# Two-layer graph network on one core: layer 2's load of the kept rows moved from SyncE's list to GpSimd's

## What is computed

```
h   = relu(layernorm(x))
w   = two-layer network on the edge features      # 192 weights per edge
msg = products of w, h[src] (through a linear map) and the edge's harmonics
agg = segment_sum(msg, dst)                       # 384 values per node
x   = x + f(h) + agg @ W_out                      # layer 1 also gates, layer 2 doesn't
```

## Time and profile before

| what | value |
|---|---|
| median of 3 runs | 2381.24 us (2380.62 to 2384.26) |
| the profiled execution, its own time | 2395.86 us |
| its span | 2394.1 us |
| granted TensorE clock, mean | 0.97 |
| busy over the span | PE 91%, PEld 86%, ACT 81%, DVE 80%, POOL 64% |
| bytes moved | 351.30 MB, mean 147 GB/s |

### The profile page before, as it was taken

One profiled execution on the slowest core, in us unless ns is written; L12 is line 12 of the kernel. 1 busy time (PEld: TensorE's weight loads), 2 busy tenths in 40 slices (PEclk: granted clock), 3 DMA queues, 4 the chain that ended last, 5 costly groups with the idle time before them and its releaser, 6 DMA issues. The chain is left out here.

```text
span 2394.1 us, 79209 instructions
## 1 busy us (share of the span) xinstructions
PE 2184.4 (91%) x22003; PEld 2050.8 (86%) x22004; DVE 1907.2 (80%) x8636; ACT 1929.9 (81%) x5167; POOL 1528.5 (64%) x1925
## 2 busy tenths in 40 slices
PE   0899998999999999999999999569999998999997
PEld 0788888889888999899999999468999998999996
DVE  6878898789888889888889888237777776777775
ACT  2677888788888888798889989348888886888885
POOL 4866787678777887777777776144545554555551
PEclk9999999899999999999999999679999999999998
DMA  5455557644444445444444443256777775777773
GB/s 156 99 144 146 140 148 185 184 124 129 126 125 127 125 128 134 116 132 132 132 130 132 132 126 113 68 135 171 189 188 179 194 192 157 182 193 187 188 192 90
DMA packets 498819, 351.30 MB, mean 147 GB/s; under 512 B 188108, under 2 KB 484030, under 8 KB 498382
## 3 DMA queue, kind: packets, MB, share of 16 engines
q1 hardware_dynamic: 401007, 209.61, 34.2%
q0 software_dynamic: 41472, 69.42, 12.9%
q10 hardware_dynamic: 55904, 67.22, 8.1%
HBM read 199.00 MB, written 151.77 MB: 147 GB/s over the span
## 5 line engine op out<-in xcount | busy, mean ns | idle before, releaser
L1066 POOL DMA_INDIRECT xg<-table,from_row x411 | 397.4, 967 | 428.9 <-DVE msg L1239 225.4
L1628 PE MATMUL out_ps<-w_out,aggT 128*128 128x128 f32 (+1 forms) x4932 | 602.5, 272 | 19.4 <-issue 12.2
L1628 PEld LDWEIGHTS out_ps<-w_out,aggT 128*128 128x128 f32 x4932 | 589.4, 194 | 23.7 <-issue 18.8
L1066 POOL DMA_INDIRECT xg<-in_x,win x411 | 473.1, 1151 | 139.7 <-issue 120.3
L1613 PE MATMUL agg_ps<-sel,msg 128*128 128x128 f32 x3708 | 527.3, 284 | 28.9 <-issue 10.5
L1613 PEld LDWEIGHTS agg_ps<-sel,msg 128*128 128x128 f32 x3708 | 465.1, 196 | 38.2 <-issue 29.1
L1444 ACT ACTIVATE msg<-pw,win 128x64 f32<-128x64 f32 x1233 | 341.7, 353 | 5.2 <-issue 2.8
L1455 ACT COPY aggT<-agg_ps 128x768 f32<-128x768 f32 (+1 forms) x310 | 247.3, 798 | 111.4 <-PE agg_ps L1613 63.6
L1489 ACT ACTIVATE kept<-out_ps,a_sb 128x320 f32<-128x320 f32 x410 | 193.7, 524 | 51.3 <-PE out_ps L1657 39.3
L1410 ACT ACTIVATE hn<-xn,nmr,rs 128x192 f32<-128x192 f32 x411 | 201.3, 540 | 39.3 <-DVE nmr L1171 37.6
L1079 POOL TENSOR_TENSOR rs<-ve,neghalf 128x4 f32<-128x4 f32 x206 | 221.5, 1075 | 17.2
(11 more groups left out here) (194 smaller groups left out, 5047.7 us busy)
## 6 DMA issues: line engine op xcount, KB each, us to landing
base_tab<-kept ACTq DMA_DIRECT2D x205, 320.0 KB
kept<-base_tab SPq DMA_DIRECT2D x205, 320.0 KB
xn<-in_x SPq DMA_DIRECT2D x411, 80.5 KB, 1.8
table<-kept SPq DMA_DIRECT2D x410, 80.0 KB
out<-kept SPq DMA_DIRECT2D x410, 80.0 KB
ee_sb<-ee_parts SPq DMA_DIRECT2D x411, 22.5 KB, 1.7
ee_parts<-part SPq DMA_DIRECT2D x45, 196.0 KB
ee_sb<-ee_parts SPq DMA_DIRECT2D x411, 18.0 KB
```

The costliest lines, as they stand in the source:

```text
L1066: pool.indirect_dma_start(out=xg[:, t.slot, j, 0:D], out_offset=None, in_=edge_rows, in_offset=bass.IndirectOffsetOnAxis(ap=at, axis=0)).t ...
L1628: ins = pe.matmul(rows[0:NT, j, c0:c1], aggT[:, t.half, j, k, :], w[f"out{k}_"][:, :], start=fresh, stop=True, skip_group_check=not fresh)
```

## The change

In layer 2, SP no longer issues the load of the kept rows in its step n. POOL issues it in step n+1, behind the gathers of turn n+2, with the same wait for `base_added`, the same source, destination and semaphore.

```diff
@@ sync, step(T)
-                if (t := T(0)) and not first:
-                    hold(sp, base_added, t.freed_m(RING))
-                    sp.dma_start(kept[:, t.slot, :, D:KEPT], base_tab[t.n]).then_inc(xn_in[t.slot], 16)
@@ gpsimd, step(T)
                 if t := T(-1):
                     gather(t)
+                if (t := T(1)) and not first:
+                    hold(pool, base_added, t.freed_m(RING))
+                    pool.dma_start(kept[:, t.slot, :, D:KEPT], base_tab[t.n]).then_inc(xn_in[t.slot], 16)
```

## The result

The changed kernel is faster: 2340.05 us (median of 4 runs, 2336.71 to 2348.72) beside 2380.93 for the kernel before (4 runs, 2374.80 to 2384.26). The ratio is 0.9844, 95% interval [0.9812, 0.9877]. The forecast of 2382 with no change was wrong, and 2340 lies outside its range too. The profiled execution has a span of 2339.1 us, where that of before had 2394.1.

A forecast was written before the change was run, and what follows sets the result against it. The prediction took the ring of PE, ACT and DVE, 3.74 us a turn, as layer 2's bound. Zeros for SP, POOL, the load and the start summed to no change, 2382 us; range 2366 to 2445.

The forecast's parts named there:

- the ring of PE, ACT and DVE: Layer 2: these three engines wait for each other and set the turn at 3.74 us; SP and POOL follow.
- the slower stretches: Parts of layer 2 with turns of about 4.55 us or more, 26 us together; cause not told by the trace.
- Every term that I had at 0: Costs and gains for SP, POOL, the load itself and the start, each counted as 0 us.
- What leaves SP: SP's list in layer 2: one load issue a turn, 0.53 us, 109 us in all; gain 0.
- My own last line: Closing sign of being wrong: a layer 2 pace below 3.7 us would mean that SP counted after all.
- X: Time of POOL's new load request in layer 2, taken as 1.02 us; hidden up to 1.06.
- The lower bound: Least time for POOL's new request: SP's 0.53 us for the same transfer.
- POOL becomes the bound: Slower rival, chance 0.34: from X = 1.06 POOL's layer 2 turn sets the pace, 2436 to 2545 us.
- P: POOL's layer 2 turn, two gathers, three gaps and the load: 3.85 us, hidden by slack up to 3.89.
- Stretched beside DVE: Slower rival, chance 0.04: POOL's request lengthens beside DVE's work, at worst losing 346 us, to 2727.
- The start and the slower stretches shrink: Faster rival, chance 0.20: up to 6 us at the start, 26 in layer 2; half, 16 us, gives 2365.
- What would show it: Signs in the later profile: load on POOL's queue, request near 1.02 us, gathers near 0.97, layer 2 pace 3.74.

The follow-up runs named there:

- e6c: Kernel before with layer 2's gathers left out of its main pass, SP's load kept: 2316.53 us beside 2393.20, ratio 0.9706, in a held session.
- e1: Kernel before with SP's layer 2 load of the kept rows left out on every engine: 2371.41 us beside 2378.29, ratio 0.9972, held session.
- e3c: Changed kernel with POOL loading 304 of 320 columns and SP again requesting the other 16: 2380.69 us beside 2389.95, ratio 0.9961, held session.
- after_c: The changed kernel, nothing altered, run again in a held session beside the kernel before: 2361.27 us, ratio 0.9877.
- e5: Kernel before plus POOL memsets of 1152 unused columns behind its gathers each turn, no added DMA: ratio 1.0071 in a free session.
- e7: Changed kernel with POOL loading only 16 of 320 columns and SP none: ratio 1.0009 beside 2293.27 us, in a free session.
- e4d: Kernel before with SP loading 304 columns and POOL the other 16 as a third request: 2383.90 us beside 2393.20, ratio 0.9961, held session.

## Why the prediction was wrong

**The step that failed** is the first: "the ring of PE, ACT and DVE sets the turn; SP and POOL follow it", with 3.74 us as the ring's own pace. PE's own turn is 3.50 us (e6c, and the kernel before in a free session). The other 0.24 us a turn and the slower stretches were PE's signals held beside POOL's gathers. I read ACT's 0.63 us in the earlier trace rows as PE and ACT waiting for each other. What should have stopped me stood in the same view: PE's sums were over, ACT was idle, and a wait for a finished producer needs a third party. PE's own wait of 0.39 us in that view ended in "issue", not in anything of ACT. The row of POOL's gather, ending 0.68 us ahead of the copy, stood close by. Every term that I had at 0 was worked out against a pace that was itself the thing to be gained.

**What leaves SP, 0.** Right for e1, within its interval (0.9972, up to 1.0000). Wrong inside the change: with SP's small request back, e3c loses most of the gain that after_c has beside it. My own last line had it: a pace below 3.7 "would mean that SP counted after all". It counted, but not by the 0.53 us that it takes on SP's list. That SP waits for the rows that it stores was also thin: 28 waits in 205 turns.

**X.** 0.746 us, not 1.02. Taking it from how a gather's time grows with its rows was the wrong neighbour: a direct request of 256 runs is cheaper than a gather of 128, and stands nearer to SP's 0.53. The lower bound was the better guide. The gaps were right at 0.30, except that the load follows the gather with none. The gathers took 1.03 us, over the 1.0 that I had set as a sign of being wrong, but the kernel before has 1.01 in a free session without any new request. So POOL's turn is about 2 x 1.03 + 0.746 + 2 x 0.30 = 3.41 us by the means, and 3.50 in the rows below (first gathers start 3.50 us apart, 1899.00 and 1902.50), and not 3.85.

POOL's own rows of one turn in the changed kernel:

```profile
1899.00 1.20 POOL L1063 DMA_INDIRECT xg<-table,from_row  x1 [0.30 <-issue]
1900.51 0.95 POOL L1063 DMA_INDIRECT xg<-table,from_row  x1 [0.30 <-issue]
1901.45 0.74 POOL L1094 DMA_DIRECT2D kept<-base_tab  x1
1902.50 1.21 POOL L1063 DMA_INDIRECT xg<-table,from_row  x1 [0.30 <-issue]
```

**POOL becomes the bound, 0.34.** It didn't. The mechanism is real, as e5 shows, but its threshold was wrong by as much as the pace was. Against 3.50 us POOL's new turn has nothing to spare, where I had credited it with P up to 3.89.

**Stretched beside DVE, 0.04.** Not seen: none of the 205 new requests takes over 0.780 us. The Trainium skill (SBUF — State Buffer, SBUF: two separate sides, the box on the "DVE blocks DMA" trap) ties the stretching to VectorE operations in a two-port mode, and whether DVE's operations in layer 2 are of that kind no run here shows.

**The start and the slower stretches shrink, 0.20.** The direction is this rival's, and the size is not: the median fell by 41 us where the rival had 16, and 32 with all of it. The 26 us in the slower stretches all went, and so did part of the 0.24 us a turn, for which the rival had no term; that it was the one that came nearest is partly luck. At the start, the first L1163 comes 13.7 us behind the first gather and not 22.6, 9 us where I allowed 6. With SP's load in its place the kernel before takes 13.4 there in a free session, so this too was a hold-up and not a crowd on the DMA engines. "No wait in them names SP or a load" was true, and worth less than I made of it, since they ended "remote", that is, unexplained.

**What would show it.** Right: the issue row, q0's bytes, POOL's wait for messages under 40 (22.3), 8 tenths. Wrong: the mean near 1.02, the gathers near 0.97, the gap of 0.30 ahead of the load, the pace of 3.74.

**What is shown and what stays open.** Shown: without layer 2's gathers that layer has no hold-ups, at other times there are none with gathers either, and then the change gains nothing (0.9999). Either half of the change alone gains 0.4% at most, the whole 1.2 and 1.6%. Not shown: what holds the signals, what makes a session held or free (the same program on the same chip met both), and whether the third thing that goes with the change, 320 KB in POOL's queue, has a part beside the two halves; e7 might have told it in a held session. That SP's requests during a pair of gathers make a long hold-up fits the ten long waits of before and the zero of after, but e1, with no load on SP, still had three.

## What to carry to other kernels

Where an idle engine starts later than the end of its producer, the pace isn't yet the ring's own: work out what the producer's own turn is before costing anything at zero against it, and look at what the other engines do in the gap; here it was GpSimd's gathers. Let the kernel before stand beside every run and look at its time each time: here it moved by some 4% with nothing changed, and an effect of 1.6% came and went with it. A gain of that kind is worth having, but it is no gain in the kernel's own work.

## What the runs showed of the hardware

- In held sessions PE's signals and SP's instruction stream are late beside gathers of GpSimd. The copies that wait for them start 0.4 to 1.0 us behind the gather's end (94 of 104 late copies in the kernel before, 98 of 98 in e1, 128 of 130 in e4d), and over a pair DVE waits 3.1 to 3.2 us. It is the record of the semaphore's update that comes late (1803.77 for sums over at 1802.93); without gathers, or in a free session, it stands 0.01 us behind the sums. In free sessions there is not one late copy in layer 2, with the same gathers.
- Whether a signal is held goes by the gather's place: 429 of 475 copies are late where the sums end within 0.1 us of a gather's end, 7 of 297 where they end over 0.5 us behind it.
- That condition is worth some 4% of this kernel: 2378 to 2393 us against 2293 to 2294.
- A direct request of 256 runs takes GpSimd 0.746 us with 1,280 B a run and 0.744 with 64 B a run in e4d: the bytes don't count. No run varies the number of runs.
- Delaying the gathers by a later wait didn't change where they fall against PE (0.22, 0.21 and 0.12 us ahead of the sums' end).
